# Relative logits in eight 64-row, 32-column tiles, relative products in column tiles, and the W2 products six steps behind instead of four

## The reference

```python
h = concatenate([tokens(x), txt], axis=1)
qkv = group_norm(layernorm(h) @ W_qkv)
logits = einsum('bhdi,bhdj->bhij', q, k) + einsum('bhdi,dij->bhij', q, rpe_k) + einsum('bhdi,dij->bhij', k, rpe_q)
attn = softmax(logits)
out = einsum('bhij,bhdj->bhdi', attn, v) + einsum('bhij,dij->bhdi', attn, rpe_v)
h = h + group_norm(out)
out = sum over 2 gates, 8 experts of gelu((layernorm(h) * p_i) @ W1 + b1) @ W2 + b2
```

## Time and profile before

| | before |
|---|---|
| median of 3 runs | 2934.63 us (2927.7 to 2934.8) |
| the profiled execution | 2932.71 us |
| its span on the core | 2930.8 us |
| mean granted TensorE clock | 0.994 |
| PE busy | 2862.8 us, 98% of the span |
| DVE, ACT, POOL busy | 67%, 67%, 35% |

### The profile page before, as it was taken

The page is one execution under the profiler, slowest core; times in us unless marked ns, Lnnn a source line. Parts: engine busy times, 40 slices in busy tenths (PEclk is TensorE's granted clock), DMA queues, the critical chain, the costliest instruction groups (busy, mean ns, idle before and its releaser), DMA issues.

```text
span 2930.8 us, 65392 instructions
## 1 busy us (share of the span) xinstructions
PE 2862.8 (98%) x21348; PEld 2294.8 (78%) x21348; DVE 1975.8 (67%) x4885; ACT 1957.8 (67%) x4640; POOL 1025.8 (35%) x999
## 2 busy tenths in 40 slices
PE   6998899999999999999999999999999999999998
PEld 6996777777777778777777777777777787777776
DVE  4665666776676667666666666666766676666665
ACT  4564467776766667766666677766666677666666
POOL 0000233434333434434333334444333344343334
PEclk9999999999999999999999999999999999999999
DMA  9994011111111011111110111111110111111100
GB/s 184 213 207 137 17 31 36 31 36 36 34 33 32 15 36 31 36 36 36 31 36 19 28 36 31 36 36 36 31 34 13 36 31 36 36 36 31 33 9 12
DMA packets 104390, 134.79 MB, mean 46 GB/s; under 512 B 10110, under 2 KB 98750, under 8 KB 99902
## 3 DMA queue, kind: packets, MB, share of 16 engines
q1 hardware_dynamic: 97442, 131.00, 19.8%
q10 hardware_dynamic: 6896, 3.09, 0.5%
HBM read 118.97 MB, written 15.07 MB: 46 GB/s over the span
## 4 chain that ended last, share of the span: by engine, by line
PE 83%; ACT 7%; DVE 4%; issue 3%; DMA 2%; SPq 1%; POOL 0%; DVEq 0%; ACTq 0%; POOLq 0%
PE bank L398 20%; PE bank L407 7%; PE bank L499 6%; PE bank L553 6%; PE bank L552 6%; PE bank L520 6%; PE bank L408 6%; PE bank L411 6%; PE bank L585 4%; ACT arena L949 4%; PE bank L506 4%; PE bank L534 3%; PE bank L562 2%; DVE mx L745 1%; SPq L339 1%
## 5 line engine op out<-in xcount | busy, mean ns | idle before, releaser
L1014 POOL TENSOR_TENSOR arena<-arena 128x386 f32<-128x386 f32 x672 | 734.5, 1100 | 710.4 <-ACT arena L893 702.5
L892 ACT ACTIVATE arena<-bank,b_s 128x386 f32<-128x386 f32 x1024 | 596.0, 582 | 445.5 <-DVE arena L614 396.0
L398 PE MATMUL bank<-arena,w_s 128*128 128x386 f32 x2048 | 831.2, 490 | 0.3 <-POOL arena L1014 0.2
L614 DVE TENSOR_TENSOR arena<-bank,ratio 128x386 f32<-128x386 f32 x1024 | 571.2, 559 | 269.0 <-PE bank L411 247.4
L893 ACT ACTIVATE arena<-arena,b_s 128x386 f32<-128x386 f32 x1024 | 623.2, 609 | 0.0
L407 PE MATMUL bank<-x_hi,w_hi 128*128 128x386 f32 x1024 | 577.2, 564 | 2.5 <-ACT x_hi L965 1.8
L949 ACT ACTIVATE arena<-bank,mx 128x193 f32<-128x193 f32 x800 | 325.9, 425 | 163.9 <-DVE mx L745 163.9
L398 PEld LDWEIGHTS bank<-arena,w_s 128*128 128x128 f32 x2048 | 369.1, 190 | 20.9 <-POOL arena L1014 10.6
L408 PE MATMUL bank<-x_hi,w_lo 128*128 128x386 f32 x1024 | 350.2, 342 | 0.0
L411 PE MATMUL bank<-x_lo,w_hi 128*128 128x386 f32 x1024 | 348.8, 341 | 0.0
L499 PE MATMUL bank<-rw,arena 128*128 128x193 f32 x1600 | 318.5, 339 | 4.1 <-DVE arena L735 3.9
(11 more groups left out here) (155 smaller groups left out, 4215.1 us busy)
## 6 DMA issues: line engine op xcount, KB each, us to landing
a_rep<-u_scratch SPq DMA_DIRECT2D x32, 1600.0 KB, 9.8
arena<-in_x SPq DMA_DIRECT2D x192, 196.0 KB
g_bc<-g_scratch SPq DMA_DIRECT2D x64, 193.0 KB, 3.6
hk<-in_txt SPq DMA_DIRECT2D x32, 128.0 KB, 2.5
u_scratch<-k_f SPq DMA_DIRECT2D x32, 100.0 KB, 2.2
u_scratch<-q_f SPq DMA_DIRECT2D x32, 100.0 KB, 2.2
out<-o_s SPq DMA_DIRECT2D x64, 48.5 KB
out<-o_s SPq DMA_DIRECT2D x64, 48.0 KB
```

Of the source, the lines that this page charges most:

```text
L398: mm(yb[:, 0:T2], w2_s[:, f, :], gelu1[:, f % RING, :], start=(f == 0), stop=(f == NF - 1)).then_inc(S["w2_done"], 1)
L614: v.tensor_tensor(gelu2[:, f % RING, :], zb[f % 2][:, 0:T2], ratio[:, :], ALU.mult).then_inc(S["z2_done"], 1)
L892: a(gelu1[:, f % RING, :], zb[f % 2][:, 0:T2], ACT.Gelu, bias=b1_s[:, f:f + 1]).then_inc(S["g_done"], 1)
L1014: g.tensor_tensor(gelu1[:, f % RING, :], gelu1[:, f % RING, :], gelu2[:, f % RING, :], ALU.add).then_inc(S["pool_sum"], 1)
```

## The change

- **Relative terms of the logits.** The rows of an octet are split by query half (rows 0 to 3 and 4 to 7 of the octet) and by image. Where one full 128x128 product stood, four tiles of 64 rows by 32 columns stand: the half sets the 64 contracted rows, image and half the 32 output rows. In a pair of fills the eight tiles of two octets follow one another. `a_bd` and `a_rep` have half the columns. A tiny F32R product of two columns with a zero operand (`carrier`) opens each bank, so that all tiles accumulate.
- **Octets of a fill** are o and o + 2 instead of o and o + 1.
- **A new DVE item `halve`** copies q and k into `u_f`, split by half, and `spread` issues four writes and two reads where it issued two and one.
- **Relative products.** Per octet and chunk there are two products of 64 columns of `rv` with the 64 columns of `pr` of one query half, placed at columns 0 and 64 of the array. `pr` is ordered image, half, head, row.
- **W2** is six steps behind; six `~w2t` stand in the turn's head. `SCHEDULE` is a new order: 14 `C` and 14 `c` steps where 11 and 17 stood, `nv`, `grow`, `~otr` and others moved.
- Masks and index orders follow (`mask_i` and a new `mask_q`, `head`), the copies of `tr` name the new axes of `pr` over the same bytes, and the waits on `a_spread` count two transfers.

```diff
-RW = 2 * L - 1
+RW = 2 * L + 3
+LH = 4 * (OCT + 1)
...
-LAG = 4
+LAG = 6
...
-EARLY = "st1 txt nb1 xt1 proj gmean gvar gaff nqk swap nv".split()
+EARLY = "st1 txt nb1 xt1 proj gmean gvar gaff nqk halve swap nv".split()
...
-    "qs0 ~grow ~w2t vt ~w2t am0 log0 am1 ~w2t qs1 log1 ~w2t qs2 am2 log2 qs3 log3 ~ot am3 log4 log5 ~hres ~bcast log6 log7 qs4 ~xin hkeep log8 log9 log10 ~otr log11 log12 txt tr0 ~a st1 tr1 ~a rel0 ~a tr2 rel1 nb1 tr3 inv rel2 tr4 rel3 tr5 rel4 ~ocopy tr6 xt1 rel5 ~a c rel6 proj pv0 rec0 gmean c pv1 rec1 gvar place0 place1 C gaff c omean c c C C nqk ovar C c C C oaff onorm C oh2 c swap mean2 C var2 nv top C c gate C C c c c c c c c gate2 c c"
+    "~w2t vt am0 ~grow qs0 ~w2t ~w2t log0 ~w2t ~w2t am1 qs1 am2 log1 log2 log3 ~w2t ~ot log4 log5 am3 log6 qs2 ~hres log7 ~bcast ~xin ~otr hkeep log8 qs3 log9 log10 qs4 txt log11 log12 st1 tr0 ~a tr1 rel0 ~a ~a tr2 ~a rel1 C ~ocopy tr3 inv C rel2 tr4 nb1 rel3 C tr5 C rel4 tr6 xt1 rel5 rel6 proj pv0 gmean c rec0 c gvar pv1 rec1 place0 place1 C gaff c omean C C nqk ovar C C halve C C oaff onorm c c oh2 c mean2 swap C C var2 top c c c gate C c c c c nv gate2 c"
...
+def octets(i):
+    return [o for o in (4 * (i // 2) + i % 2, 4 * (i // 2) + i % 2 + 2) if o < OCT]
...
-    o = min(2 * i + 1, OCT - 1)
-    return sum(o >= c for c in cuts[1:])
+    return sum(octets(i)[-1] >= c for c in cuts[1:])
...
-        k_f, k_sw = (sb(n, [P, LP]) for n in ("k_f", "k_sw"))
+        k_f = sb("k_f", [P, 7 * 32])
+        k_sw = sb("k_sw", [P, LP])
+        carrier = sb("carrier", [P, P], F32R)
+        u_f = sb("u_f", [P, 2, 2, LH])
...
-        a_rep = sb("a_rep", [P, BH, LP])
+        a_rep = sb("a_rep", [P, BH, LH])
...
-        arena = sb("arena", [P, 2 * RING * T2 + 3 * OCT * P + OCT * P // 2 + OCT * L])
+        arena = sb("arena", [P, max(2 * RING * T2 + 3 * OCT * P + OCT * L, PATCH * (P + NTOK * (1 + XT)))])
...
-        q_bd = part(OCT * P // 2).rearrange("p (o b r) -> p o b r", b=H, r=8)
-        a_bd, *pr = (part(OCT * P).rearrange("p (o b r) -> p o b r", b=BH, r=8) for _ in range(3))
+        q_bd = part(OCT * P // 2).rearrange("p (m h r) -> p m h r", h=H, r=4)
+        a_bd = part(OCT * P // 2).rearrange("p (o b r) -> p o b r", b=BH, r=4)
+        pr = [part(OCT * P).rearrange("p (o i e h r) -> p o i e h r", i=2, e=2, h=H, r=4) for _ in range(2)]
...
-                sp.wait_ge(S["norm"], t * 4 + 2)
-                for src, x in enumerate((k_f, q_f)):
-                    sp.dma_start(u_scratch[src, :, :, :].rearrange("d b i -> b d i"), x[:, 0:LP]).then_inc(S["u_out"], 16)
-                sp.wait_ge(S["u_out"], t * 32 + 32)
-                sp.dma_start(a_rep[:, :, :], u_scratch[:, :, :, :].rearrange("s d b i -> (s d) (b i)").unsqueeze(1)
-                             .broadcast_to([2 * DK, 8, BH * LP])).then_inc(S["a_spread"], 16)
+                for half in range(2):
+                    sp.wait_ge(S["halved"], t * 4 + 2 * half + 2)
+                    for src in range(2):
+                        sp.dma_start(u_scratch[half, src, :, :, :].rearrange("d b i -> b d i"), u_f[:, half, src, :]).then_inc(S["u_out"], 16)
+                sp.wait_ge(S["u_out"], t * 64 + 64)
+                for half in range(2):
+                    sp.dma_start(a_rep[64 * half:64 * half + 64, :, :], u_scratch[half, :, :, :, :].rearrange("s d b i -> (s d) (b i)").unsqueeze(0)
+                                 .broadcast_to([4, 2 * DK, BH * LH])).then_inc(S["a_spread"], 16)
...
-                        for k in range(2 if 2 * i + 1 < OCT else 1):
-                            o = 2 * i + k
-                            mm(lt[(i + 2) % LOGS][:, k * 256:k * 256 + L], a_bd[:, o, :, :], rw[:, 192 - 8 * o:192 - 8 * o + L], start=(k == 0), stop=False, skip_group_check=True)
+                        mm(lt[(i + 2) % LOGS][:, 510:512], carrier[:, :], carrier[:, 0:2], start=True, stop=False, skip_group_check=True)
+                    for k in range(2):
+                        for half in range(2):
+                            for img in range(2):
+                                for i in both:
+                                    rows = slice(64 * half, 64 * half + 64)
+                                    rh = half ^ (i % 2)
+                                    to = 64 * img + 32 * rh
+                                    for o in octets(i)[k:k + 1]:
+                                        x0 = 196 - 8 * o - 4 * rh
+                                        mm(lt[(i + 2) % LOGS][to:to + 32, 256 * k:256 * k + L], a_bd[rows, o, 8 * img:8 * img + 8, :], rw[rows, x0:x0 + L],
+                                           start=False, stop=False, skip_group_check=True, tile_position=(64 * half, to))
...
+                                for o in octets(i)[k:k + 1]:
+                                    m = mm(lt[(i + 2) % LOGS][to:to + 64, k * 256:k * 256 + L], q_bd[rows, 2 * o:2 * o + 2, :, :], (k_sw if i % 2 else k_f)[rows, 0:L],
...
-                                    if half == 1 and (k == 1 or 2 * i + 1 == OCT):
+                                    if half == 1 and o == octets(i)[-1]:
...
-                                       pr[c][0:jn, :, H * b + hh, :], start=False,
+                                       pr[c][0:jn, :, b, :, hh, :], start=False,
...
-                        part = pv[g % 2][:, (o - octs[0]) * P:(o - octs[0] + 1) * P]
-                        mm(part, rv[:, (8 * o + P) * HD:(8 * o + P) * HD + P], pr[0][:, o, :, :], start=True, stop=False)
-                        m = mm(part, rv[0:JC[1][1], 8 * o * HD:8 * o * HD + P], pr[1][0:JC[1][1], o, :, :],
-                               start=False, stop=True)
+                        for c, (j0, jn) in enumerate(JC):
+                            w = (8 * o + (0 if c else P)) * HD
+                            for half in range(2):
+                                m = mm(pv[g % 2][64 * half:64 * half + 64, (o - octs[0]) * 64:(o - octs[0]) * 64 + 64],
+                                       rv[0:jn, w + 64 * half:w + 64 * half + 64], pr[c][0:jn, o, :, half, :, :],
+                                       start=(c == 0), stop=(c == 1), skip_group_check=True, tile_position=(0, 64 * half))
...
+                elif s == "halve":
+                    dve.wait_ge(S["norm"], t * 4 + 2)
+                    if not is_first(t):
+                        dve.wait_ge(S["u_out"], t * 64)
+                    quads = lambda x: x[:, :].rearrange("p (m e r) -> p m e r", e=4, r=4)[:, 0:13, :, :]
+                    to = lambda part, src: u_f[:, part, src, :].rearrange("p (m e r) -> p m e r", e=2, r=4)
+                    for part, cut in ((0, slice(0, 4, 3)), (1, slice(1, 3))):
+                        for src, x in enumerate((k_f, q_f)):
+                            v.tensor_copy(to(part, src), quads(x)[:, :, cut, :]).then_inc(S["halved"], 1)
...
-                                    a_rep[:, :, 8 * o0:8 * o1].rearrange("p b (o r) -> p o b r", r=8),
-                                    K["mask_q"].unsqueeze(1).unsqueeze(1).broadcast_to([P, o1 - o0, BH, 8]),
+                                    a_rep[:, :, 4 * o0:4 * o1].rearrange("p b (o r) -> p o b r", r=4),
+                                    K["mask_i"].unsqueeze(1).unsqueeze(1).broadcast_to([P, o1 - o0, BH, 4]),
...
-                    v.tensor_tensor(wm[:, g * GRP:g * GRP + w, :, :],
-                                    pv[g % 2][:, 0:w * P].rearrange("p (o b r) -> p o b r", o=w, r=8),
-                                    K["mask_r"].unsqueeze(1).unsqueeze(1).broadcast_to([P, w, BH, 8]),
+                    v.tensor_tensor(wm[:, g * GRP:g * GRP + w, :, :].rearrange("p o b (h r) -> p o b h r", h=2),
+                                    pv[g % 2][:, 0:w * 64].rearrange("p (o b r) -> p o b r", o=w, r=4).unsqueeze(3).broadcast_to([P, w, BH, 2, 4]),
+                                    K["mask_r"].rearrange("p (h r) -> p h r", h=2).unsqueeze(1).unsqueeze(1).broadcast_to([P, w, BH, 2, 4]),
...
+                v.memset(carrier[:, :].bitcast(F32), 0.0)
...
-                    a4 = lambda x: x.rearrange("p (m e x) -> p m e x", e=2, x=16)
+                    a4 = lambda x: x.rearrange("p (m e x) -> p m e x", e=2, x=8)
...
-                        a(a4(q_mix[there, :])[:, 0:6, 1, :], a4(q_f[here, :])[:, 0:6, 1, :], ACT.Copy).then_inc(S["exchanged"], 1)
+                        a(a4(q_mix[there, :])[:, 0:12, 1, :], a4(q_f[here, :])[:, 0:12, 1, :], ACT.Copy).then_inc(S["exchanged"], 1)
...
-                    for k in range(w):
-                        o = 2 * i + k
-                        m = a(lp[:, o, 0:L], lt[(i + 2) % LOGS][:, k * 256:k * 256 + L], ACT.Exp, bias=mx[:, o:o + 1],
+                    for k, o in enumerate(octets(i)):
+                        m = a(lp[:, o, 0:L], lt[(i + 2) % LOGS][:, k * 256:k * 256 + L], ACT.Exp, bias=mx[:, 2 * i + k:2 * i + k + 1],
...
-                c0 = 126 - r
```

(27 more changed lines are left out.)

6 lines of the change are left out of this document (1 added, 5 removed).

## The result

The changed kernel takes 2973.66 us (median of 3 runs, 2965.22 to 2975.15) against 2934.63: 1.0133 of before, 95% interval 1.0096 to 1.017. It is slower, and lies outside the forecast's range around 2770 us. The profiled execution took 2965.22 us, with a span of 2963.3 and a mean granted clock of 0.962.

A forecast was written before the change was run, and what follows sets the result against it. PE was taken to bound the kernel. Terms 3.6 + 1.8 - 0.4 + 0.2 - 0.1 gave 5.1 us per turn, 32 times 163 us, off 2932.7: 2770 us; range 2735 to 2850.

The forecast's parts named there:

- Relative products, +3.6 per turn: Column tiles side by side in rel: 5.6 us where 11.1 stood, less 1.95 for changes of tiling; gain 3.6.
- Logits' tiles +1.8: Eight tiles at once make a pair of fills 1.98 us against 2.32; less the last fill's loss, gain 1.8 per turn.
- masks +0.2: Halved a_bd and W2 products as cover shorten PE's waits for am at the fills; gain 0.2 us per turn.
- halve -0.1: Four extra DVE copies, 0.8 us, between nqk and oaff among eight steps C or c; 0.1 us lost per turn.
- Chain -0.4: Maxima and exponentials behind the logits delay tr0's second half and rel0; loss 0.4 us per turn (0 to 1.0).
- order and W2 at 0: W2 six steps behind moves two products from the feed-forward to the turn's head, work for work; counted at 0.
- Masks to "about 0.6": With a_bd halved, DVE's mask am0 goes from 1.14 to about 0.6 us, the other masks alike.
- Sum 5.1 per turn: All terms over one turn, 3.6 + 1.8 - 0.4 + 0.2 - 0.1 = 5.1 us gained, 32 times 163 us.
- The turn of 78 us: Sign that the forecast is right: turns of 78 us, where a turn took 83.1 before.
- Four tiles at once: Rival: in the logits only four 64x32 tiles run at once, a pair takes 8 slots; 2891 us, chance 0.10.
- a pace of issue: Rival: PE can't sustain more than one matmul per 0.04 us in logits and rel; 2957 us, chance 0.06.
- DVE holding the feed-forward: Rival: DVE ends last in steps C12 to C17, costing 2 us per turn; 2834 us, chance 0.10.

The follow-up runs named there:

- e13: Kernel before with relative products in column tiles, new order and W2 six behind, full logits products, all turns written out: 2821.84 us, 0.9624.
- e1: Changed kernel with its 29 looped turns written out, same order, waits and tiles: 2771.93 us, 0.9438 of the kernel before.
- e9: Kernel before with the new order (without halve) and W2 six behind, full products, all turns written out: 2945.25 us, 1.003.
- e5: Changed kernel with only PE's turns written out, the other engines looped: 2811.62 us, 0.958 of the kernel before.
- e2: Kernel before with two turns in the loop's body, same operations and order: 2978.91 us, 1.0138.
- e6: Changed kernel with only DVE's turns written out, the other engines looped: 2949.04 us, 1.0057 of the kernel before.
- e14: Changed kernel with PE's and DVE's turns written out, ACT, POOL and SP looped: 2775.63 us, 0.9461 of the kernel before.
- e4: Changed kernel with the relative products full again, looped; logits' tiles, new order and W2 six behind stay: 2931.74 us, 0.9976 of the kernel before.

## Why the prediction was wrong

The terms of the sum held nearly, and a term was missing.

- *Relative products, +3.6 per turn.* With the full logits (2929.9 - 2827.2) / 32 = 3.2 in the old order, which is what the forecast's own prices give there, and (2945.3 - 2821.8) / 32 = 3.9 in the new; with the logits in tiles (2911.4 - 2771.9) / 32 = 4.4. Right, a little low.
- *Logits' tiles +1.8, masks +0.2, halve -0.1: +1.9.* 1.56 by `e13` against `e1`, and 1.76 by their windows of one turn. Eight tiles run at once, the pair takes 1.94 us where 1.98 was worked out, and halve costs 0.08. Right in the new order; in the old one 0.1 is left by the medians, and no term foresaw that.
- *Chain -0.4, order and W2 at 0.* The chain's loss is there, but it belongs to the order and not to the tiles: at the transposes PE waits 23.3 us for ACT in `e9` and `e13`, with full logits, and 13.4 in `e1`. Order and W2 with full products are (2929.9 - 2945.3) / 32 = -0.5. Right in size, put down to the wrong part.
- *Masks to "about 0.6".* `am0` takes 0.76 us in `e1`, above the forecast; the median of the four falls from 1.02 to 0.55.
- *Sum 5.1 per turn.* Written out on both sides, (2929.9 - 2771.9) / 32 = 4.9. That `e1` lands at 2771.9, beside the forecast's 2770, has some luck in it: 6 us of it come from writing out by itself.
- **The step that failed is the sum itself: "3.6 + 1.8 - 0.4 + 0.2 - 0.1 = 5.1 us, 32 times".** It counted the new records only by the time that each takes on the array (200 for the relative products, 32 per pair of fills), and not what their number does to the loop around them. In its place the runs showed: 526 more instructions in PE's turn, 39%, and 11 in DVE's push both bodies out of their stores, which costs 7.2 us per jump (162 of the 202 us by PE, `e5`), more than the 5.1 that the tiles save. The turn of 78 us that was to show the forecast right is there written out (77.7) and stands in the loop as 84.7. The row to look at was on the page before the change: instruction queues nearly empty (34 and 18 packets) in a kernel that is looped.
- *The rivals.* Four tiles at once and a pace of issue are both excluded: 32 tile records start within 0.56 us, eight of them 0.007 apart and then a step of 0.12 to 0.14. DVE holding the feed-forward doesn't occur in the changed order (0.08 us a turn); in the old order it does (0.76). The pace of issue was the rival of the other side and came nearest in kind (too many instructions), but its place was wrong: the price is paid at the jump and not per product.

Shown: the jump's cost (`e1`), its dependence on the body's size alone (`e2`), its split between PE and DVE (`e5`, `e6`, `e14`), and that 1663 PE instructions still fit (`e4`). Only argued: that the fall of the clock makes the 78 us by which PE's busy time is longer, since no run has the gaps without the fall. Open: why PE's reload has two gaps, the second inside L457, why a reload fetches 10 packets for a body that takes 7 written out, and whether for DVE the size of 273 to 278 instructions decides or where the body begins in its store.

The version that beats both kernels is the changed one written out, `e1`, at 2771.9 us, 5.6% under before.

## What to carry to other kernels

Count the instructions that a change adds to each engine's loop body, beside their time: splitting products into tiles multiplies them. Look at the instruction queues on the page and for waits on "issue" that stand once per turn; if both are there, write the loop out (or make the body smaller) before judging the change. Where a kernel written out is compared with a looped one, write out the kernel before as well. An order written by hand and the size of its products belong together: tiles that were worth 3 us in one order were worth 50 in another.

## What the runs showed of the hardware

- PE keeps a loop body of 1663 instructions across a jump and doesn't keep one of 1863 (10 packets of 16 KB per turn; 2.3 and 2.1 us idle in the mean, 64.6 and 58.9 over 28). The Trainium skill (Runtime: NRT & Kernel Launch, "Instruction fetch mechanics") gives PE a store of 2048 instructions, refilled in blocks of 256. The packets agree, and the limit seen lies somewhat below that size.
- The same section of the Trainium skill warns that a taken branch whose target isn't in the current window of two pages forces a fetch before execution goes on. That stall is what the trace shows after the change. But with two such pages the kernel before, of 1337 instructions, would have had it too, and its 34 packets say that it had not.
- DVE keeps 273 and reloads at 278 (5 packets of 8 KB per turn, 2.2 us idle).
- A reload costs more than its gap: the granted clock was 0.50 for 3 to 7 us behind it in each turn of the changed kernel, while the mean clock of `e2` stayed at 0.988 (0.962 in the changed kernel).
- Tiles of 64x32 in both row halves wrote the same banks with eight running at once: 32 records in 0.81 us with the change of tiling.
